# A two-layer block on one core: filler products between the mixing weight products, four weight transfers moved ahead of a wait, and a narrower wait before the quantised products

## The reference

```python
h = gelu(embedding @ W0 + b0); h = gelu(h @ W1 + b1)
att = softmax(h @ W2 + b2)                      # 64 x 8
agg_w = einsum('bk,koi->boi', att, weight)      # one 32 x 32 matrix per batch
out = einsum('boi,bih->boh', agg_w, x) + (att @ bias_k)[:, :, None]

def _qlinear(x, q, scale, A, Bm):
    w = (q - 7.5) * (scale * 0.005)[:, None]
    return einsum('bsh,oh->bso', x, w) + 0.02 * (x @ A @ Bm)
g = _qlinear(x, gate...); u = _qlinear(x, up...)   # 512 -> 1376, rank 32
return _qlinear(silu(g) * u, down...)              # 1376 -> 512
```

## Time and profile before

| | |
|---|---|
| Median of 3 runs | 375.7 us (375.58 to 376.06) |
| Span of the profiled execution | 375.1 us |
| Around the span, by the median | 0.6 us |
| PE busy | 365.7 us, 97% of the span |
| DVE, ACT, POOL busy | 246.0, 190.5, 93.1 us |
| PE's granted clock, mean | 0.995 of full speed |

### The profile page before, as it was taken

One profiled execution on the slowest core, in us unless ns is written; L12 is line 12 of the kernel. 1 busy time (PEld: TensorE's weight loads), 2 busy tenths in 40 slices (PEclk: granted clock), 3 DMA queues, 4 the chain that ended last, 5 costly groups with the idle time before them and its releaser, 6 DMA issues.

```text
span 375.1 us, 5791 instructions
## 1 busy us (share of the span) xinstructions
PE 365.7 (97%) x2208; PEld 302.5 (81%) x2208; DVE 246.0 (66%) x399; ACT 190.5 (51%) x345; POOL 93.1 (25%) x78
## 2 busy tenths in 40 slices
PE   8999999999999999999999999999999999998994
PEld 3777887899888888998888889998888899997331
DVE  3858999727476665263766652547889922588995
ACT  4557698403555554134565550235667511066972
POOL 2101432411133224111323232113223321142030
PEclk9899999999999999999999999999999999999999
DMA  7599676197320000142200000526000199977288
GB/s 218 178 228 367 193 264 215 54 336 154 53 44 0 0 0 3 22 64 42 43 0 2 2 0 2 83 36 160 0 3 1 48 287 268 197 163 180 92 174 276
DMA packets 82475, 41.72 MB, mean 111 GB/s; under 512 B 52416, under 2 KB 72784, under 8 KB 82320
## 3 DMA queue, kind: packets, MB, share of 16 engines
q1 hardware_dynamic: 69072, 37.70, 37.2%
q10 hardware_dynamic: 12624, 1.82, 3.1%
q0 software_dynamic: 752, 1.84, 2.5%
HBM read 26.55 MB, written 14.80 MB: 110 GB/s over the span
## 4 chain that ended last, share of the span: by engine, by line
PE 82%; DVE 7%; ACT 4%; DMA 2%; issue 2%; POOL 0%; DVEq 0%
PE ps L675 34%; PE ps L660 24%; PE ps L608 4%; PE ps L690 4%; PE ps L710 3%; PE ps L868 3%; DMA x_nat<-in_gate_q 2%; PE ps L568 2%; PE ps L666 2%; PE ps L712 2%; ACT mix L937 1%; PE ps L848 1%; DVE a_buf L1423 1%; PE ps L623 1%; ACT h_hi L979 1%
## 5 line engine op out<-in xcount | busy, mean ns | idle before, releaser
L1137 POOL TENSOR_TENSOR h_lo<-a_buf,h_hi 128x512 fp32r<-128x512 f32 (+1 forms) x44 | 57.5, 1307 | 121.6 <-ACT h_hi L979 121.6
L660 PE MATMUL ps<-down_w,h_hi 128*128 128x288 f32 (+1 forms) x352 | 76.2, 297 | 0.4 <-POOL h_lo L1137 0.4
L660 PE MATMUL ps<-down_w,h_lo 128*128 128x288 f32 (+1 forms) x352 | 74.8, 293 | 0.0
L675 PE MATMUL ps<-x_hi,gate_w 128*128 128x512 f32 (+1 forms) x176 | 69.9, 397 | 0.0
L675 PE MATMUL ps<-x_hi,up_w 128*128 128x512 f32 (+1 forms) x176 | 69.7, 396 | 0.2 <-DVE b_buf L1416 0.2
L675 PE MATMUL ps<-x_lo,gate_w 128*128 128x512 f32 (+1 forms) x176 | 69.6, 396 | 0.0
L675 PE MATMUL ps<-x_lo,up_w 128*128 128x512 f32 (+1 forms) x176 | 69.3, 393 | 0.0
L660 PEld LDWEIGHTS ps<-down_w,h_hi 128*128 128x128 f32 (+1 forms) x352 | 57.2, 189 | 1.7 <-POOL h_lo L1137 0.6
L660 PEld LDWEIGHTS ps<-down_w,h_lo 128*128 128x128 f32 (+1 forms) x352 | 56.1, 188 | 0.0
L1423 DVE TENSOR_TENSOR a_buf<-a_buf,b_buf 128x512 f32<-128x512 f32 (+1 forms) x44 | 50.0, 1136 | 8.9 <-ACT a_buf L1043 7.8
L1147 POOL TENSOR_TENSOR x_nat<-y_buf,x_nat 128x512 f32<-128x512 f32 x15 | 20.8, 1385 | 94.8 <-DVE y_buf L1309 94.8
(11 more groups left out here) (194 smaller groups left out, 492.7 us busy)
## 6 DMA issues: line engine op xcount, KB each, us to landing
x_nat<-in_x SPq DMA_DIRECT2D x4, 1024.0 KB, 7.1
out<-x_nat SPq DMA_DIRECT2D x15, 256.0 KB, 4.3
turned<-x_nat SPq DMA_DIRECT2D x12, 256.0 KB, 3.3
x_nat<-in_down_q SPq DMA_DIRECT2D x11, 256.0 KB, 3.4
x_nat<-in_gate_q SPq DMA_DIRECT2D x10, 256.0 KB, 7.4
x_nat<-in_up_q SPq DMA_DIRECT2D x10, 256.0 KB, 7.4
edges<-zeros SPq DMA_DIRECT2D x4, 512.0 KB, 9.3
xt_own<-turned SPq DMA_DIRECT2D x6, 256.0 KB, 3.5
```

The lines of the kernel that those rows point to most:

```text
L660: last = mm(ps[:, 4 + 2 * (j % 2) + m, 0:HALF + R], part[0:k, ic, j * P:(j + 1) * P], down_w[0:k, ic, m, :], start=first, stop=end)
L675: last = mm(ps[0:k, bank(ic, 2 * m), :], w[:, H * ic + c * k:H * ic + (c + 1) * k], part[:, c, :], start=c == 0 and part is x1_hi, stop=c ...
L1137: nc.gpsimd.tensor_tensor(h_lo[0:k, ic, :], a_buf[0:k, ic % 2, :], plain(h_hi[0:k, ic, :]), ALU.subtract).then_inc(h_lo_ready, 1)
```

## The change

It does four things.

1. In the opening, `keep_clock` takes a number of columns. One filler of 128 columns stands ahead of the mixing weight products, one of 192 columns (BETWEEN) between each two of them (seven), and one of 256 columns behind the four fillers ahead of `condition(0)`.
2. SP issues slots 4 to 7 ahead of its waits for B, where slots 4 and 5 stood behind the store of B, and slots 6 and 7 behind its two loads.
3. `quantised(t, ic, m)` for ic from 2 waits for ACT's eviction of the chunk two before (`ag_ready`, `au_ready`). The wait for DVE's sum (`g_ready`, `u_ready`) stands behind it, ahead of `low_rank`.
4. In the last tile's chunk 5, the spread of the weight maximum into the low rank bank gets a wait for `g_ready` of its own.

```diff
+BETWEEN = 192
@@ SP
             sp.dma_start(stage_mask[:], batch_mask).then_inc(ctx_in, 16)
+            for n in range(4, RING):
+                load_slot(n)
             sp.wait_ge(lrb_hi, 1)
             sp.wait_ge(lrb_ready, 1)
             sp.dma_start(lr_b_rows..., plain(lr_b_parts[:])).then_inc(lrb_stored, 16)
-            for n in range(4, 6):
-                load_slot(n)
             sp.wait_ge(lrb_stored, 16)
             for half in range(2):
...
-            for n in range(6, RING):
-                load_slot(n)
@@ PE
             keep_clock(WARM[4])
+            keep_clock(1, P)
...
             for o in range(S // OB):
                 last = mm(ps[:, MIX_BANK, o * B:(o + 1) * B], cond_w_parts[:, o, :], att_parts[:], start=True, stop=True)
+                if o < S // OB - 1:
+                    keep_clock(1, BETWEEN)
...
             keep_clock(4)
+            keep_clock(1, HALF)
             pe.wait_ge(mix_ready, 2)
             condition(0)
...
-                        pe.wait_ge((g_ready, u_ready)[m], t * IC + ic - 1)
+                        pe.wait_ge((ag_ready, au_ready)[m], t * IC + ic - 1)
                         if t == TILES - 1 and ic == W_SPREAD and m == 0:
                             pe.wait_ge(wmax, 1)
+                            pe.wait_ge(g_ready, t * IC + ic - 1)
                             spread(W_ALL, ps[:, bank(ic, 1), 0:P], w_row_mm)
                         if t > 0 or ic > 2 or m > 0:
                             quantised(t, ic, m)
...
+                        pe.wait_ge((g_ready, u_ready)[m], t * IC + ic - 1)
                         low_rank(t, ic, m)
```

More of the change, by code:

```diff
@@ L563, in _, with keep_clock @@
             mm = nc.tensor.matmul
-            def keep_clock(n):
+            def keep_clock(n, columns=TILE):
                 for _ in range(n):
-                    mm(ps[:, 7, :], warm_ones[:, 0:P], warm_ones[:], start=True, stop=True)
+                    mm(ps[:, 7, 0:columns], warm_ones[:, 0:P], warm_ones[:, 0:columns], start=True, stop=True)
             pe.wait_ge(const_set, 2)
```

## The result

The changed kernel takes **378.35 us** (median of 4 runs, 377.19 to 379.43) against 375.69 (375.58 to 376.06): a ratio of **1.0069** with an interval of 1.0051 to 1.0088. It is slower, by 2.7 us. The prediction was 375.2, with a range up to 376.2: wrong, and on the wrong side. Run again among the experiments, as `e9_changed_again`, it took 378.21 against 376.07 (1.0059, interval 1.0034 to 1.0084).

What follows compares the result with a forecast made beforehand. It took tile 0's elementwise chain, started by the later of PE and B, to bound the kernel. A start 0.38 us sooner plus 0.11 from slot 8 gave 0.5: span 374.6, median 375.2 us, range 374.2 to 376.2.

Steps and rivals of the forecast that it cites:

- The price of a pair: Opening: a mixing product plus filler takes 0.18 us instead of 0.12, so seven and the leading filler delay 0.47 us.
- the fillers cost their bound: Rival, chance 0.10: at 0.34 us a pair the opening is 1.6 us late, giving 376.3, or 376.7 us.
- The filler's purpose: Opening: added fillers keep PE's clock at 2.4 GHz through `condition(0)`, saving PE 1.70 us.
- the clock falling all the same: Rival, chance 0.18: fillers don't hold PE's clock in the opening, PE arrives at 30.22, time stays 375.7 us.
- The chain: Tile 0: elementwise steps on DVE, ACT and POOL set the end, so starting them sooner is worth its full time.
- the later of PE and B: First low rank product, tile 0: starts when both PE's stream and B's landing are done; 29.74 instead of 30.12.
- The clock has no worth where B ends last: Opening: PE ready at 28.58, B at 29.68, so most of PE's 1.7 us is spent waiting for B.
- The transfers: Opening: slots 4 to 7 issue free, B's store lands 0.85 us sooner, B's loads stay at 9.0.
- Slot 8: Tile 0: this slot lands at least 1 us sooner, so DVE's 0.11 us wait for it goes.
- The narrower wait: PE's 0.16 us wait for DVE's sum at 32.16 goes but is given back at 73.69: worth 0.
- POOL against DVE: Opening: if DVE's conversion of slot 2 goes ahead of POOL's step on B, B is 0.35 us late.
- From span to median: Whole kernel: the median lies 0.6 us above the span, so 374.6 gives 375.2 us.

Runs made afterwards that it cites:

- e9: The changed kernel run again unaltered, beside the kernel before: 378.21 us against 376.07, ratio 1.0059.
- e14: The changed kernel with its seven fillers between mixing products on rows 32 to 63, which those products don't use: 376.10 us (one run).
- e1: The kernel before with only the nine opening fillers added, transfers and waits as before: 379.37 us against 376.26, ratio 1.0080.
- e13: The changed kernel with its seven fillers between mixing products on rows 0 to 63 instead of 128 rows: 379.75 us (one run).
- e7: The changed kernel with 64 columns instead of 192 in each filler between mixing products: 379.06 us, ratio 1.0070.
- e10: The changed kernel without the five fillers ahead of `condition(0)`, those between mixing products kept: 378.20 us, ratio 1.0049.
- e2: The kernel before with only slots 4 to 7 issued ahead of the waits for B: 375.91 us, ratio 0.9988.
- e3: The kernel before with only the waits of `quantised` and of the spread changed: 375.86 us, ratio 0.9989.
- e8: The changed kernel with its seven fillers of 192 columns moved ahead of the mixing products: 375.90 us, ratio 0.9992.
- e12: The changed kernel with fillers between mixing products on 32 rows and B's loads cut into 2.75 KB packets: 375.99 us, ratio 0.9998.

## Why the prediction was wrong, point by point

**The price of a pair: this step failed.** I took 0.18 us, and 0.34 as the bound if nothing hid. Both are too small, since the bound added 0.14 for the filler's load to a pitch of 0.12 that already had the mixing product hidden under its neighbour's load. With nothing overlapped a pair is two loads (0.18 and 0.10) and two products one behind the other, 0.41 measured. The row that I took as nearest was the wrong neighbour. Its 32 products go round four separate blocks of 32 rows (0 to 31, 32 to 63 and so on), the cheap case of e14, where the fillers alternate between 128 and 32 rows that they share. The four filler loads of 0.14 in the earlier trace rows were fillers among themselves, of equal rows. The close trains of before with unlike rows that share some were those of 96 beside 128, which cost nothing; none had 32 beside 128, and I priced it as if one did. The rival "the fillers cost their bound" was what happened, and its break-even of 0.25 us a pair was passed; it had a chance of 0.10 and ended at 376.7, too low by 1.6 us.

**The filler's purpose: wrong in part.** I gave 0.18 to the clock falling all the same. In the profile of the changed kernel it fell, at 12.94 for 3.42 us; in e9's it held. It also fell for longer: the mean granted clock was 0.986 to 0.991 in 7 of the 14 executions of the changed kernel (spans 377.2 to 378.7) and 0.994 or more in the rest (375.0 to 375.9). 0.990 or less stands in 6 of the 14, and in none of the 91 of before. Against the median span of 374.4 in before, the 7 with the fuller clock have a median 1.0 us longer and the other 7 one of 3.2: all lose 1 us, and half of them some 2 us more. Two executions of that kind have a profile, e1's and e13's, and in both the half-speed stretch is 6.8 us instead of 3.4 (e13: from 12.0 to 18.9). There the tail fillers run at half speed throughout and `condition(0)` starts 1.4 and 1.7 us after the copies of `mix`, against 0.8 in the changed kernel's profile. A line of e13:

```profile
14.00:15.00 1.00, 1.00 (x4) 0.43 (x3) 0.88 (x3) 0.98 (x3) 0.00 (x0) 0.50 1.04 399
```

The runs show that a mean of 0.990 or less comes with the steps of 0.36 and 0.41 alone (also in e1, e7, e10 and e13); why it comes there, and only in some executions, stays open. The low clock isn't all of it either: one of e1's six has a span of 377.3 at a mean clock of 0.998.

**The chain: held.** From DVE's first low rank sum to PE's down products it is 42.9 to 43.0 us in before (30.73 to 73.69) and changed (31.29 to 74.19), and in e1 (34.56 to 77.48), 4 us later. Whatever delays that sum delays the end, and "the later of PE and B" decided it: B in before, e2, e3, e8, e9 and e12, PE in the changed kernel's profile, in e1 and in e13. From Sum to the end of the span it is 344.2 to 345.3 us in all 17 profiles of the table.

**The clock has no worth where B ends last: held**, by e3. With B sooner, my sum gave a full clock 0.48 us (29.74 against 30.22); e8 and e9 show 0.4 and 0.7.

**The transfers.** The four issues ran at 9.55 to 11.40, free, as said. The store gained 0.56, where I took 0.85: mis-sized. The loads of B, which I left at 9.0 for each, came 0.5 to 0.8 us sooner in e8 and e9 (9.23 and 9.20 from issue to product, where before took 9.77 and e3 9.98), but not in e2 (9.83): the low end of 0 to 0.6 was one of the answers. Slot 8 went out at 24.31 instead of 25.97 and nobody waited for it. None of it moved the median.

**The narrower wait: held.** I said 0; e3's ratio is 0.9989 with 1 in the interval.

**POOL against DVE: open, and harmless.** In e3 DVE's conversion of slot 2 took 1.81 us where it takes 0.42 alone, and POOL's step on B (13.58 to 15.23) its usual 1.65:

```profile
13.70 1.81 DVE L1212 TENSOR_SCALAR gate_w<-x_nat 128x512 fp32r<-128x512 int32 x1
```

POOL had started 0.12 sooner. It was first, by 0.11 to 0.12 us, in every profile with a full clock (e3, e8, e9, e12), so the 0.35 that I held against B was never paid.

**From span to median.** I added 0.6 us to the span. In every later run, of every kernel, the time is 1.7 to 2.1 us above the span; before's profiled execution, with its span of 375.1, was one of its longer ones (of the 91 later ones 85 lie at 373.6 to 375.4, with the median at 374.4). For a difference this cancels, but a median forecast from one profile carries that spread, here more than the 0.5 us forecast.

With the pair at 0.41, the store at 0.5 and the loads at 0.78, the same working gives +0.8 us with the clock held. The right answer was "slower" by that step alone, and the executions with the fuller clock bear it out (1.0 us). The measured 2.1 to 2.7 us needs the long stretch at half speed on top, whose cause is not shown.

## What to carry to other kernels

A filler between small products of 32 rows was cheap on the same rows as they use, or on another 32: here 0.16 and 0.11 us a step, against 0.41 with 64 or 128 rows that take theirs in. Before pricing a matmul that is put between others, look in the trace for a pair with the same two row sets, not for the same type or size; and if none is there, take as the bound both loads and both products in series. And ask first whether the engine that is to be sped up ends last: B did in before, so that a full clock was worth nothing there and 0.7 us at most once B came sooner, while the fillers put 2.0 us ahead of B.

## What the runs showed of the hardware

- Weight loads were hidden under the product before where both use the same rows (0.12 us a step, fp32r after fp32r; 0.16 for bf16 and fp32r together) or separate blocks of 32 rows (0.11), and also between 96 and 128 rows that share 96 (0.27 for two products, as without the change). They were not hidden between 32 rows and 64 or 128 that take them in (0.41, bf16 fillers between fp32r products).
- The clock fell although PE had not been idle for more than 0.2 us at a time since 7.82 in the changed kernel (it fell at 12.94) and since 3.72 in e1 (at 13.90), where it came back only after 6.8 us in which PE was busy throughout.
- Executions of one kernel differ by 1 to 2 us (before: spans of 373.8 to 376.1 on one chip), and the profiles differ in when the clock is low and when the mixing starts (8.8 to 10.4 us, with no fillers' doing: before 9.89, e3 8.81). One profile can't settle a difference of that size.
